# The place of the index-list copy in the second layer of a graph network on one Trainium2 core

## The reference

```
s_u = x @ W_u.T + b_u ;  s_v = x @ W_v.T
e = s_u[src] + s_v[dst] ;  e = where(e >= 0, e, 0.2 * e)
m = segment_max(e, dst)
e_exp = exp(e - m[dst])
denom = segment_sum(e_exp, dst)
out = segment_sum(x.reshape(N, 32, 8)[src] * (e_exp / denom[dst])[:, None, :], dst)
x = layernorm(x + out)
```

## Time and profile before

| what | us |
|---|---|
| median of 3 executions | 4930.07 (4929.89 to 4938.38) |
| the profiled execution: its time | 4929.81 |
| the profiled execution: its span, first to last instruction | 4928.1 |
| first index copy of layer 1 | 3213.8 |
| scores of the first group begin | 3258.7 |
| scores of the last group begin | 4823.1 |

### The profile page before, as it was taken

How to read it: one execution, slowest core, us unless ns; L and a number is a source line. 1 busy time by engine, 2 the same in 40 slices (tenths; PEclk the granted TensorE clock), 3 DMA queues, 4 the chain that set the end, 5 groups by cost and what they waited for, 6 DMA issues and landing times. The chain is left out here.

```text
span 4928.1 us, 61408 instructions
## 1 busy us (share of the span) xinstructions
PE 3099.3 (63%) x13554; PEld 1900.6 (39%) x13555; DVE 2202.6 (45%) x5019; ACT 908.4 (18%) x2810; POOL 3434.9 (70%) x2948
## 2 busy tenths in 40 slices
PE   3547877777777777877778768834444444444441
PEld 1224444444444444444444435523333333333331
DVE  2543333333333333333333349855555555555554
ACT  0212222222222222222222223300000000000002
POOL 4238888888888888888888867756666666666564
PEclk9869898888998888888898889956666666666665
DMA  7777767667767677677677666643333333333332
GB/s 285 193 241 137 135 126 136 133 123 135 132 126 138 127 131 134 126 135 132 123 136 132 123 133 206 181 148 93 95 92 100 93 94 91 96 98 94 92 93 66
DMA packets 471760, 641.52 MB, mean 130 GB/s; under 512 B 173608, under 2 KB 365636, under 8 KB 467887
## 3 DMA queue, kind: packets, MB, share of 16 engines
q0 software_dynamic: 198144, 339.26, 36.4%
q1 hardware_dynamic: 245994, 254.83, 17.6%
q10 hardware_dynamic: 27588, 47.08, 3.0%
HBM read 448.23 MB, written 192.71 MB: 130 GB/s over the span
## 5 line engine op out<-in xcount | busy, mean ns | idle before, releaser
L935 POOL DMA_INDIRECT S<-l_msum,l_sink x784 | 1280.7, 1634 | 254.2 <-issue 213.5
L1466 POOL DMA_INDIRECT l_feats<-X_rows,l_gsrc x880 | 1008.1, 1146 | 605.6 <-DVE l_gsrc L1574 340.7
L918 POOL DMA_INDIRECT l_ga<-A_rows,l_gsrc x784 | 791.3, 1009 | 265.6 <-issue 155.4
L1008 PE MATMUL l_psU<-l_hid,l_same 128*128 128x257 f32 x1568 | 585.0, 458 | 534.7 <-ACT l_hid L1044 518.2
L981 PE MATMUL l_psC<-l_table,l_onehot 128*128 x4728 | 726.5, 295 | 0.0
L1532 PE MATMUL l_psU<-l_feats,l_same 128*128 128x264 f32 x1760 | 555.7, 481 | 146.5 <-DVE l_feats L1699 129.2
L1048 ACT COPY l_msum<-l_psU 128x257 f32<-128x257 f32 x784 | 292.6, 373 | 1883.8 <-POOLq L934 1296.1
L974 PE MATMUL l_psC<-W1cT,l_attrT 64*128 64x256 f32 x1576 | 619.0, 476 | 13.1 <-DMA l_table<-B_rows 13.1
L981 PEld LDWEIGHTS l_psC<-l_table,l_onehot 128*128 128x128 bf16 x4728 | 426.0, 104 | 364.9 <-issue 303.4
L1008 PEld LDWEIGHTS l_psU<-l_hid,l_same 128*128 128x128 f32 x1568 | 266.1, 213 | 669.9 <-ACT l_hid L1044 598.9
L1532 PEld LDWEIGHTS l_psU<-l_feats,l_same 128*128 128x128 f32 x1760 | 413.8, 242 | 281.8 <-issue 189.2
(11 more groups left out here) (346 smaller groups left out, 3512.2 us busy)
## 6 DMA issues: line engine op xcount, KB each, us to landing
l_srcb<-src_rows SPq DMA_DIRECT2D x99, 512.0 KB
l_locb<-lo_rows SPq DMA_DIRECT2D x55, 512.0 KB
S<-su_zeros ACTq DMA_DIRECT2D x24, 1156.5 KB
l_locb<-loc_rows SPq DMA_DIRECT2D x99, 256.0 KB
nd_sums<-S SPq DMA_DIRECT2D x196, 128.5 KB, 2.2
l_attr<-in_edge_attr SPq DMA_DIRECT2D x98, 256.0 KB
GH_rows<-l_hidden SPq DMA_DIRECT2D x49, 384.0 KB
nd_hidden<-GH_rows SPq DMA_DIRECT2D x49, 384.0 KB, 3.2
```

The source lines that it names most:

```text
L918: pool.indirect_dma_start(ga[:, s, :], None, D["A"], bass.IndirectOffsetOnAxis(ap=gsrc[h][:, j % HALF:j % HALF + 1], axis=0)).then_inc(gat ...
L935: pool.indirect_dma_start(D[f"S{j % NTAB}"], bass.IndirectOffsetOnAxis(ap=sink[j // HALF][:, j % HALF:j % HALF + 1], axis=0), msum[:, j % ...
L1008: nc.tensor.matmul(psU[j % 2][:, 0:UW], same[j // HALF][:, j % HALF, :], hid[:, j % RING, :], start=True, stop=True).then_inc(agg_done, 1)
L1466: pool.indirect_dma_start(feats[r][:, t, :], None, D["X1"], bass.IndirectOffsetOnAxis(ap=gsrc[r][:, t:t + 1], axis=0)).then_inc(gathered[r ...
```

## The change

The call of `stage_index(g + SETS, r)` goes from the end of DVE's body to its beginning, under the same condition. Nothing else is changed: the copy writes the same list into the same buffer, the number and order of all other instructions is the same, and `find_edge` (L1581) and the weight products (L1699) go on reading both of their operands from SBUF.

```diff
                 c = Chain(dve, dve_step, base)
                 at = bass.ds(g * GROUP, GROUP)
 
+                if not isinstance(g, int) or g < XG - SETS:
+                    stage_index(g + SETS, r)
                 if not last:
                     find_node(g + 1, 1 - r)
                 if not first:
...
                 if not last:
                     take_scores(g + 1, 1 - r, c)
                     local_max(g + 1, 1 - r, c)
-                if not isinstance(g, int) or g < XG - SETS:
-                    stage_index(g + SETS, r)
                 if first:
                     steps["first"] = c.n
```

## The result

The changed kernel took 4686.26 us, the median of 4 executions (4682.95 to 4708.66), against 4930.58 us before: a ratio of 0.9508, 95% interval 0.9482 to 0.9535. The forecast was 4647 us, inside a range of 4601 to 4713. The gain was put at 283 us and is 244.

What follows compares the result with a forecast made beforehand. Layer 1 was taken as a closed loop of DVE and POOL, 29.11 us a group; less POOL's 5.86 us wait, plus a 0.30 gap and 0.30 new stalls, 23.85 over 53 groups gains 282.8 us: 4647 us, range 4601 to 4713.

Steps and rivals of the forecast that it cites:

- The closed loop: Layer 1: DVE waits for POOL's rows (5.94 us a group), POOL for DVE's list copy (5.86); period 29.11 us.
- The copy costs nothing: DVE in layer 1: the moved 0.17 us copy leaves the steady instruction sequence the same, cost 0.
- the buffers are free in time: POOL's wait for summed buffers costs nothing: free at T+16.65 after scores start at T, reached about T+22.
- from the other side: Buffer check: even if POOL began only at T+16.65, rows would land at T+42.4, due at T+47.7.
- POOL's bound, 23.85 us: Layer 1 after the change: POOL's 16 gathers without a pause, 23.55 us plus 0.30 of new stalls, set the period.
- Landing: Layer 1: DVE starts the scores 1.92 us after the last gather ends, unchanged by the edit.
- VectorE's bound, 23.17 us: DVE's layer 1 period without its wait for rows, 29.11 - 5.94; 0.7 us below POOL, so not binding.
- The wait that was left for DVE: Layer 1 after the change: DVE's wait for gathered rows shrinks to 0.5 to 1 us a group.
- Rival 3: Gathers block seven DVE instructions in POOL's former pause, 0.95 us each: period 29.8 us, 4967 us; chance 0.03.
- the stall term: POOL's gathers newly meeting L1578 and small two-SBUF-operand DVE instructions lose 0.30 us a group.

Runs made afterwards that it cites:

- e1: Changed kernel, but with the list copy late in the body, just ahead of the next scores and their wait for rows: ratio 0.9523 to the kernel before.
- e3: Kernel before (copy at the end) with the comparison's column numbers and the product weights read from PSUM: 4728.9 us, ratio 0.9645.
- e2: Changed kernel with the comparison's column numbers and the product weights read from PSUM: 4590.7 us, ratio 0.9367 to the kernel before.
- e10: Kernel before (copy at the end) with only the comparison's column numbers read from PSUM: 4842.3 us, ratio 0.9863.
- e9: Changed kernel with the comparison's column numbers in PSUM and the copy moved to just ahead of the scores: 4646.6 us, ratio 0.9458 to the kernel before.
- e4: Changed kernel with 12 of 16 gathers in each group from the third on, part of the gathering left out: ratio 0.9337 to the kernel before.
- e6: Changed kernel with only the comparison's column numbers read from PSUM, copy at the top: 4910.96 us, ratio 0.9961 to the kernel before.

## Why the prediction was right, and where 39 us went

*The closed loop.* Right, by the waits, by e1, and by two pairs each on one chip (e3 and e2, e10 and e9): the copy had to leave the far side of DVE's wait for rows, and where in front of that it stands matters little.

*The copy costs nothing; the buffers are free in time.* Right for the regular groups: DVE's busy time rose by 0.2 us a group (2202.6 to 2213.4 over the span), and POOL's waits for `agg_done` were under 0.6 us but for a few. The check "from the other side" has a slip: by its own terms POOL's rows would land 23.85 + 1.92 = 25.8 us after T+16.65, not 27.4; the T+42.4 that it arrives at is right for 25.8.

*POOL's bound, 23.85 us.* Measured 24.04 in 51 undisturbed groups and 24.01 in all 53 of the second trace. The mean gather, forecast at 1.16 to 1.19 us, was 1.181 and 1.176. The first of these makes 0.56 us a group more than the 1.146 of before, where I had 0.30: of the sum's terms the new stalls were sized too small, by 0.26 us a group, some 14 us in all (by the second trace 0.18 and 10).

*Landing.* Taken as 1.92 us. In the 24 groups of the first trace in which VectorE waited for rows, it started 1.85 us (median) after the end of the last gather.

*VectorE's bound, 23.17 us.* Measured by e2 (23.24) and e4 (23.00), both on chip 0. The wait that was left for DVE, forecast at 0.5 to 1 us a group, was 0.6 and 1.1. That it lies only some 0.8 us below POOL would explain why in the first trace about half of the groups show no wait at all; this is argued, not shown.

*Rival 3, gathers that hold VectorE up.* Not in the form that I gave it. L1578, which now meets gathers, went from 0.753 to 0.821 us on average: 0.07 us. The rule of the Trainium skill that I had set against the rows ("SBUF — State Buffer", section "SBUF: two separate sides") holds in the direction in which GpSimd waits for VectorE. I had left out its conditions: on VectorE's side it names only instructions in a two-port mode, or with two SBUF inputs, the latter only against a GpSimd instruction that reads SBUF. So it would not have blocked all seven instructions of Rival 3: L1598, for one, reads one of its operands from PSUM. In the other direction these runs show tenths of a microsecond, not whole gathers, but not nothing. In the kernel before, L1670 began 0.45 to 0.46 us into a gather in 20 of its 55 runs; it then took 475 to 486 ns and ended within 0.02 us of the gather's end. Where it began 0.04 to 0.22 us into a gather (23 times) it took 218 to 220 ns. So from about its middle on a gather held L1670, while L1581 kept its length.

*What no step had.* The late starts after TensorE. In the first trace two groups lost 8.2 and 13.7 us beyond the others, 22 of the 39 us; 3.7 is the later start of layer 1; about 14 is the stall term. That these two are the same thing as in e6 is likely (VectorE and POOL wait for TensorE's sums there) but not shown, as records of TensorE are missing in both stretches. The changed kernel's second set of runs took 4664.66 us in the median, 18 above the forecast, and its trace has no such group; how far the first result lies from the forecast is thus in part chance. The common 0.95 us after L1519 costs little: VectorE is in L1581 meanwhile.

*Open.* What holds TensorE up in the first pair and on chip 13 and not on chips 0 and 14, and whether e6 would run at e9's speed on chip 0 or 14. The semaphores went up late, but whether the matmuls ended late or only their signals did, the trace can't tell, as it models their ends. It can be the chip, or the recording, which lost a fifth of TensorE's semaphore updates in just those traces.

## What to carry to other kernels

Look for two waits of equal length that answer each other once per pass: they are one loop, and the cheapest cut is to move the producer's release ahead of the wait on the far side, by however little. After the cut, look at whether the new bound runs without a pause, and compare the start of each engine that waits for TensorE with TensorE's end.

Before two runs are compared, compare stages that the edit doesn't touch. Here the start of layer 1 (3230 to 3242 us on two chips, 3259 to 3268 elsewhere) told two kinds of traces apart. The column numbers in PSUM cost 5% on one chip, with the copy at the top, and gained 1.4% on another, with the copy at the end; which of the two differences decides was not settled, since both were changed at once. A ratio to the kernel before on the same chip takes out a chip that is slower, but not one that reacts otherwise to the edit. A run that is to test an explanation has to be made where the effect was seen.

## What the hardware showed unexpectedly

In the first changed trace and on chip 13, with POOL running on, ScalarE started 0.8 to 1.2 us (median) after TensorE's modelled end in four of five kernels, and in the fifth, e6, VectorE started 6.65 us after it, at worst 8.6. On chips 0 and 14 it was 0.04 us for ScalarE and 0.43 to 0.50 for VectorE in all eight kernels. The DMA share does not tell the two apart: 0.34 before, where neither of these starts was late, and 0.34 in e6.

A gather that begins inside L1581 or L1699, VectorE instructions with two SBUF operands, ends 0.8 us after that instruction; with one operand of both in PSUM the mean gather is 0.949 us instead of 1.146 (e3, copy at the end) and 0.960 instead of 1.181 (e2, copy at the top). In the other direction, in the kernel before, VectorE's L1670 took 0.48 us instead of 0.22 and ended with the gather when it began 0.45 us into one; when it began up to 0.22 us into one it kept its 0.22.
